# Second phase of a two-layer kernel: the 16 state products in four VectorE instructions, and new step orders

## The reference, cut to what matters

```
xa = layer_norm(x);  sx = (xa one token earlier) - xa
xxx = tanh((xa + sx*maa_x) @ maa_w1);  xm_f = xa + sx*(maa_f + xxx_f @ maa_w2_f)      # five mixes f
w = exp(-exp(time_decay + tanh(xw @ td_w1) @ td_w2))
r, k, v = xr @ Wr.T, xk @ Wk.T, xv @ Wv.T;   g = silu(xg @ Wg.T)
for t in tokens, per head:  a = k_t v_t^T;  out_t = r_t . (u*a + s);  s = a + w_t * s   # s is 16 x 16
og = group_norm(out);  x1 = x + (og * g) @ Wo.T
xc = layer_norm(x1);  xk2, xr2 = xc + (shift of xc) * ffn_k / ffn_r
result = x1 + sigmoid(xr2 @ Wfr.T) * (relu(xk2 @ Wfk.T)^2 @ Wfv.T)
```

## Time and profile before

| | |
|---|---|
| median of 3 runs | 1634.13 us (1631.69 to 1645.39) |
| the profiled execution's own time | 1638.29 us |
| its span, first to last instruction | 1636.5 us |
| busy share of the span: PE, DVE, ACT, POOL | 89%, 59%, 44%, 29% |
| mean granted TensorE clock | 0.965 |

### The profile page before, as it was taken

How to read it: one execution, slowest core, us unless ns; L and a number is a source line. 1 busy time by engine, 2 the same in 40 slices (tenths; PEclk the granted TensorE clock), 3 DMA queues, 4 the chain that set the end, 5 groups by cost and what they waited for, 6 DMA issues and landing times. The chain is left out here.

```text
span 1636.5 us, 33172 instructions
## 1 busy us (share of the span) xinstructions
PE 1455.7 (89%) x12352; PEld 1085.1 (66%) x12352; DVE 961.4 (59%) x2287; ACT 721.5 (44%) x1772; POOL 477.0 (29%) x530
## 2 busy tenths in 40 slices
PE   5999999999999998588989888889989888998865
PEld 4777777777777775376666666566656666666532
DVE  3444444444444434267787778777867867787652
ACT  3666666666666665124234423433342343334312
POOL 1211212221111110223453245224414523442230
PEclk9999999999999999599999999999999989999978
DMA  7431111111111000300000000000000000000000
GB/s 202 133 83 37 37 37 36 36 42 45 43 43 41 12 13 7 120 12 18 6 18 24 23 6 19 23 24 2 22 24 6 18 24 23 2 23 18 17 6 12
DMA packets 25664, 54.61 MB, mean 33 GB/s; under 512 B 3984, under 2 KB 6672, under 8 KB 24016
## 3 DMA queue, kind: packets, MB, share of 16 engines
q1 hardware_dynamic: 25552, 52.99, 11.3%
HBM read 42.23 MB, written 7.34 MB: 30 GB/s over the span
## 5 line engine op out<-in xcount | busy, mean ns | idle before, releaser
L900 POOL TENSOR_TENSOR rst<-rp,st 128x448 f32<-128x448 f32 x192 | 191.0, 1019 | 124.0 <-DVE st L1064 124.0
L892 POOL TENSOR_TENSOR xm<-mixed,xa 128x448 f32<-128x448 f32 x80 | 98.9, 1236 | 384.4 <-DVE mixed L993 382.7
L272 POOL TENSOR_TENSOR aT_lo<-whole,aT_hi 128x375 fp32r<-128x375 f32 x64 | 58.6, 915 | 448.4 <-ACT whole L424 445.6
L344 DVE CUSTOM_DVE_ANT_0 probs<-a_bank,unmask 112x375 f32<-112x375 f32 x256 | 126.0, 545 | 83.1 <-PE a_bank L541 72.4
L443 ACT ACTIVATE probs<-probs,least 112x375 f32<-112x375 f32 x256 | 153.8, 608 | 0.0
L350 DVE RECIPROCAL inv_rows<-sums 112x128 f32<-112x128 f32 x64 | 61.0, 953 | 155.9 <-ACT probs L443 155.9
L452 ACT COPY probsT<-a_bank 125x448 f32<-125x448 f32 x192 | 90.1, 536 | 52.1 <-PE a_bank L594 52.1
L594 PEld LDWEIGHTS a_bank<-ident_sb,probs 112*125 112x125 f32 x768 | 90.8, 188 | 30.9 <-ACT keyT L434 16.3
L594 PE MATMUL a_bank<-ident_sb,probs 112*125 112x112 f32 x768 | 99.3, 279 | 2.9 <-ACT probs L443 2.9
L993 DVE SCALAR_TENSOR_TENSOR mixed<-b_bank,vec_sb,sx 128x112 f32<-128x112 f32 x320 | 84.0, 323 | 21.0 <-PE b_bank L1476 20.9
L539 PE MATMUL a_bank<-aT_hi,wk_lo 128*128 128x376 f32 x256 | 91.3, 357 | 1.7 <-ACT keyT L434 1.7
(11 more groups left out here) (165 smaller groups left out, 3290.5 us busy)
## 6 DMA issues: line engine op xcount, KB each, us to landing
ctx_tok<-in_ctx SPq DMA_DIRECT2D x16, 750.0 KB
xT_sb<-in_xT SPq DMA_DIRECT2D x16, 224.0 KB, 9.5
x_tok<-in_x SPq DMA_DIRECT2D x16, 224.0 KB, 9.2
x_between_layers<-x_sb SPq DMA_DIRECT2D x16, 224.0 KB, 2.3
b_x<-x_between_layers SPq DMA_DIRECT2D x16, 224.0 KB, 2.8
x_post<-x_between_layers SPq DMA_DIRECT2D x16, 224.0 KB, 2.8
out_dram<-fin SPq DMA_DIRECT2D x16, 224.0 KB, 2.8
vbd<-vtok SPq DMA_DIRECT2D x208, 16.0 KB
```

The costliest lines, as they stand in the source:

```text
L344: dve.tensor_tensor_reduce(out=probs[:, g % 2, i], in0=score_bank[i][0:T, 0:TC], in1=unmask[:, m[1]], scale=-SCALE, scalar=-LOWEST, op0=AL ...
L892: pool.tensor_tensor(xm[:, f % 2], mixed[:, f % 2], xa[:, :, 1:T + 1], ALU.add).then_inc(s_xm, 1)
L900: pool.tensor_tensor(by_chunk(rst[:, j % NPROD]), by_chunk(rp[:].rearrange("p c t -> p (c t)")), state_of(j), ALU.mult).then_inc(s_pprod, 1)
```

## The change

- The tile `st` of the states and the tile `drep` of the decays are laid out with the state column outermost: [P, S, C, NB] in place of [P, C, S, NB]. The scan runs over the same 896 elements in the new order, and `drep` is filled by one ACT instruction instead of four.
- The 16 products become four, `products(m, r)`, all on DVE. Each multiplies four state columns at once, 128 x 1792 elements. POOL has no product any more. The ring has two places of four columns each, one semaphore `s_prod` counts the four instructions, and each `reduce` waits for one of them.
- The step functions of POOL, DVE, ACT and PE are written out as plain sequences without slots, in other orders. Some functions are cut in two so that their halves can stand apart (`chunk_keys`, `decay`, `copy_sums`, `residual`, `shift2`, `token_shift`). The work in them is the same. `tanh_gate` now also waits for the batch's own decay factors, and `transpose_value` for one more instruction of the earlier batch's near values.
- The program of SP is not touched.

```diff
-        drep = sb("drep", [P, C, S, NB])
+        drep = sb("drep", [P, S, C, NB])
...
-        st = sb("st", [P, C, S, NB])
+        st = sb("st", [P, S, C, NB])
...
-        rst = sb("rst", [P, NPROD, CT])
+        rst = sb("rst", [P, 2, QUAD, CT])
...
-        def state_of(j):
-
-            return st[:, :, j % QUAD * QUAD + j // QUAD, :].unsqueeze(3).broadcast_to([P, C, NB, CH])
+        def states_of(r):
+
+            return st[:, r::QUAD].rearrange("p q c b -> p q (c b)").unsqueeze(3).broadcast_to([P, QUAD, NG, CH])
...
-            def product(m, j):
-                if j == 0:
-                    pool.wait_ge(s_st, count(m, 1, 1))
-                    pool.wait_ge(s_rp, count(m, 1, 1))
-                if j >= NPROD or at_least(m, 1):
-                    pool.wait_ge(s_red, count(m, QUAD, (j - NPROD) // QUAD + 1))
-                pool.tensor_tensor(by_chunk(rst[:, j % NPROD]), by_chunk(rp[:].rearrange("p c t -> p (c t)")), state_of(j),
-                                   ALU.mult).then_inc(s_pprod, 1)
...
+                    rec_key(m)
+                if pre:
+                    mix(n, 0)
+                if more:
+                    rstd1(p)
+                if pre:
+                    mix(n, 1)
+                if post:
+                    gate_output(l, scan)
+                if pre:
+                    mix(n, 2)
+                    mix(n, 3)
+                if post:
+                    rstd2(l)
+                if pre:
+                    mix(n, 4)
+                if more:
+                    xa_state(p)
...
-            def product(m, j):
+            def products(m, r):
                 dve.wait_ge(s_st, count(m, 1, 1))
                 dve.wait_ge(s_rp, count(m, 1, 1))
-                if j >= NPROD or at_least(m, 1):
-                    dve.wait_ge(s_red, count(m, QUAD, (j - NPROD) // QUAD + 1))
-                dve.tensor_tensor(by_chunk(rst[:, j % NPROD]), by_chunk(rp[:].rearrange("p c t -> p (c t)")), state_of(j),
-                                  ALU.mult).then_inc(s_vprod, 1)
+                if r >= 2 or at_least(m, 1):
+                    dve.wait_ge(s_red, count(m, QUAD, r - 1))
+                dve.tensor_tensor(rst[:, r % 2].rearrange("p q (g s) -> p q g s", s=CH),
+                                  rp[:].rearrange("p c (b s) -> p (c b) s", s=CH).unsqueeze(1).broadcast_to([P, QUAD, NG, CH]),
+                                  states_of(r), ALU.mult).then_inc(s_prod, 1)
 
...
+                if scans:
+                    for d in range(2, CH + 1):
+                        decay_key(m, d)
+                    near_products(m, 0)
+                    prefixes(m)
+                if post:
+                    wkv_sum(l)
+                if scans:
+                    near_products(m, 1)
+                    decay_rec(m)
+                if more:
+                    stats1(p)
+                if scans:
+                    near_products(m, 2)
+                if post and at_least(n, 3):
+                    finish(later(n, -3))
+                if scans:
+                    near_products(m, 3)
+                if pre:
+                    mix(n, 0)
+                    mix(n, 1)
+                if post:
+                    centre(l)
+                if scans:
+                    scan(m)
+                    bonus_value(m)
+                    near_values(m, 0)
+                    products(m, 0)
+                    products(m, 1)
+                if post:
+                    group_norm(l)
+                if scans:
+                    products(m, 2)
+                if pre:
+                    mix(n, 2)
+                    mix(n, 3)
+                    mix(n, 4)
+                if scans:
+                    near_values(m, 1)
+                    near_values(m, 2)
+                if post:
+                    residual(l)
+                    stats2(l)
+                if scans:
+                    products(m, 3)
+                if post:
+                    apply2(l)
+                if more:
+                    apply1(p)
+                if scans:
+                    near_values(m, 3)
+                if post:
+                    shift2(l)
+                    ffn_input(l, xk2, "ffn_k", s_xk2)
+                    ffn_input(l, xr2, "ffn_r", s_xr2)
+                if more:
+                    token_shift(p)
+                if pre:
+                    gate(n)
+                if more:
+                    mix_input(p)
...
-                for c in range(C):
-                    last = act.copy(drep[:, c], prefix[:, c, 0:NB, CH].unsqueeze(1).broadcast_to([P, S, NB]))
-                last.then_inc(s_drep, 1)
+                act.copy(drep[:], prefix[:, :, 0:NB, CH].unsqueeze(1).broadcast_to([P, S, C, NB])).then_inc(s_drep, 1)
...
                     chunk_keys(m)
+                if pre:
+                    tanh_maa(n)
+                if scans:
+                    chunk_keys_decayed(m)
+                    copy_state(m)
+                    copy_keys(m)
                     spread_decay(m)
-                if pre:
-                    tanh_maa(n)
-                if scans:
-                    copy_keys(m)
+                    copy_sums(m, 0)
+                    copy_sums(m, 1)
+                if pre:
+                    tanh_td(n)
                 if post:
                     square(l)
-                if scans:
-                    copy_sums(m)
-                if post:
                     gn_rstd(l)
                 if pre:
-                    tanh_td(n)
+                    decay_rate(n)
+                    copy_value(n)
                 if post:
                     gn_affine(l)
                 if pre:
-                    decay(n)
-                    copy_value(n)
                     copy_key(n)
+                    decay_factor(n)
+                    copy_rec(n)
                 if post:
                     xc_affine(l)
-                if pre:
-                    copy_rec(n)
+                if more:
+                    xa_affine(p)
+                if pre:
                     tanh_gate(n)
-                    copy_vtok(n)
-                if pre and not is_batch(n, B - 1):
-                    xa_affine(later(n, 1))
                 if post:
                     relu_square(l)
                     receptance(l)
+                if pre:
+                    copy_vtok(n)
 
...
-                by_pool, by_vector = products(QUAD * r + QUAD - 1)
-                pe.wait_ge(s_pprod, count(m, POOL_PRODUCTS, by_pool))
-                pe.wait_ge(s_vprod, count(m, DVE_PRODUCTS, by_vector))
+                pe.wait_ge(s_prod, count(m, QUAD, r + 1))
...
-                    last = pe.matmul(out_bank[q * (P // QUAD):(q + 1) * (P // QUAD), 0:CT], collect[:, j], rst[:, j % NPROD],
+                    last = pe.matmul(out_bank[q * (P // QUAD):(q + 1) * (P // QUAD), 0:CT], collect[:, j], rst[:, r % 2, q],
...
+                if scans:
+                    transpose_keys(m)
+                if pre:
+                    maa_second(n, (0, 1))
+                if scans:
+                    chunk_sums_free(m)
+                if post:
+                    gn_mean(l)
+                if scans:
+                    chunk_sums(m)
+                    bonus(m)
+                if pre:
+                    decay_first(n)
+                if scans:
+                    attend_near(m, 0)
+                if pre:
+                    maa_second(n, (2,))
+                if scans:
+                    attend_near(m, 1)
+                if post:
+                    gn_var(l, scans)
+                if pre:
+                    decay_second(n)
+                    project(n, 1, "wv", s_vmm)
+                if scans:
+                    reduce(m, 0)
+                    attend_near(m, 2)
+                if pre:
+                    maa_second(n, (3, 4))
+                if scans:
+                    reduce(m, 1)
+                    reduce(m, 2)
+                if post:
+                    project_out(l)
+                if pre:
+                    project(n, 2, "wk", s_kmm)
+                if scans:
+                    attend_near(m, 3)
+                if pre:
+                    project(n, 3, "wr", s_rmm)
+                if post:
+                    transpose_post(l)
+                if more:
+                    transpose_x(p)
+                if scans:
+                    reduce(m, 3)
+                if pre:
+                    project(n, 4, "wg", s_gmm)
+                    transpose_value(n)
+                if post:
+                    ffn_key(l)
+                    ffn_receptance(l)
+                if more:
+                    maa_first(p)
+                if post:
+                    ffn_value(l)
```

More of the change, by code:

```diff
@@ L908, in step @@
                 if scan:
[L909 to L933, removed]
-                        pool.tensor_copy(xc[:, :, 0:1], rows[:, index(l), 0, :].unsqueeze(2)).then_inc(s_xc0, 1)
```

(39 more changed lines are left out.)

180 lines of the change are left out of this document (46 added, 134 removed).

## The result

The changed kernel takes **1697.93 us**, median of 4 runs (1697.23 to 1698.49); the kernel before, run beside it, 1639.76 us. The ratio is **1.0354** [1.029, 1.0417]. The profiled execution took 1698.49 us with a span of 1696.7 us, against 1638.29 and 1636.5 before: 60.2 us more.

The account below looks back on a forecast made before the run. PE, busy 89%, was taken as the bound, held each step through SP's queue. 1638.3 + 35 (longer steps) + 45.5 (clock) + 6 (steps 1 and 2) - 9 (last two) = 1716, as median 1712 us; range 1655 to 1745.

Parts of the forecast that it names:

- Where the wait is, and what causes it: PE before gn_mean: late copy_vtok and early stats1 meet in SP's queue, holding PE 9.4 us every step.
- V: The moment vtok is ready; b_x lands 12.46 us later, finish's first instruction ends 14.8 us later.
- What is late next: SP's queue: b_x behind 13 transfers delays stats1 and finish, closing the loop at 58.65 us a step.
- that case: Rival at gn_mean: SP's queue does not hold, steps take 49.3 us, about 1540 us in all; chance 8%.
- The four old waits: PE's waits for chunk sums, POOL product, DVE product and normalised input, 4.98 us a step, were to go.
- `reduce` 2 holds: On PE, product 2 ends at 31.8 us, wanted at 32.2: least slack, 0.4 us.
- Products: On DVE: each of 1792 elements takes at most 2.5 us, four take 10 against about 3 before.
- `ln_tok`: On DVE, rear part: 4.87 us beside POOL's products, 0.54 us once those go.
- walk of 42.35 us: PE's work from gn_mean to wfr without waits: 40.48 us plus one reduce (0.89) and bonus (0.98).
- The correction of 4.2 us: Whole kernel: the median of runs lies 4.2 us under the profiled execution, taking 1716 to 1712 us.
- The clock: PE behind its wait at gn_mean: falls to 0.50, costing 3.5 us a step, bounds 0 and 4.6.
- the first rival: At gn_mean: the same wait, but the clock hardly falls, 1663 us; chance 22%.

Follow-up runs that it names:

- the two moves alone: Kernel before with only copy_vtok put behind receptance on ACT and stats1 of the next batch ahead of finish on DVE: 1721.62 us, ratio 1.0533.
- both moves back: Changed kernel with copy_vtok returned to right behind tanh_gate on ACT and stats1 put behind centre on DVE: 1526.89 us, ratio 0.9308.
- PE kept busy: Changed kernel with eight unread matmuls on constants added on PE ahead of gn_mean's wait for the 13 transfers: 1660.56 us, ratio 1.0155.

## Why the prediction was right

It said 1712 us, 4.8% slower, in a range of 1655 to 1745; measured were 1697.93 us, 3.5% slower than the kernel before run beside it. The likeliest case, 1690 to 1727, is the one that came.

**Where the wait is, and what causes it: right.** It named `gn_mean` on the first instruction of `finish`, a stand of 9.4 us (9.30 measured), `b_x` issued 9.66 us behind the first transfer (9.66), DVE idle for about 12 us (12.35), `gn_mean` at V + 14.8 (14.87 as the mean of the 12 full steps, from the spread's start). Putting back either move takes away its share, freeing `b_x` in SP's queue does too, and the two moves alone slow the old kernel: the cause is shown, not argued. One remark of the prediction is too strong, that the rows contradict the sentence of the Trainium skill on the sequencer's time (DMA: Bandwidth & Descriptors, section "Issuing engines are not separate DMA queues"): a single issue, 0.67 us, is small beside the 2.8 us of a landing, and only the 13 in a row are not.

**What is late next: right.** With both moves back, PE does not stand at all in the full steps. The step was added up piece by piece (walked) at 49.3 us and measures 48.57. The time given for that case, 1540, was 13 us too long.

**The four old waits go, `reduce` 2 holds: right.** No such wait is left from 820 to 1560 us. **Products: right within the bound**; the upper end of 2.5 us was taken, 2.02 measured, as by the formula of the Trainium skill that the prediction cites (VectorE: DVE Perf Modes, section "The TRN2 errata"). **`ln_tok`: the sign was right, the size not**: 1.40 us in the row above instead of 0.54, and still far from 4.87; it cost nothing, since PE waits for something else.

**The pace, term by term**, mean of the 13 steps from 810.95 to 1602.37:

| term, us | predicted | measured | from |
|---|---|---|---|
| V to `gn_mean` | 14.8 | 14.53 | 12 steps at 14.87, the last, which loads no `b_x` any more, 10.47 |
| `gn_mean` to `wfv` at full clock | 44.18 | 43.46 | predicted 42.35 and `maa_first` 1.83; 886.15 to 929.61 with PE kept busy, clock 1.00 |
| slow clock in it | 3.5 | 3.12 | mean of the 13 in the changed kernel, 46.58, less 43.46 |
| `wfv` to the next V | -0.33 | -0.23 | the starts in SP's and PE's timelines |
| step | 62.15 | 60.88 | |

The split between the second and third row is rough: 43.46 is one full step, and the last of the 13 has less work (41.00 with PE kept busy). Over the same 13 steps the changed kernel's span is 3.27 us longer than with PE kept busy, where the clock fell in one step too.

So 13 steps came out 13 x 1.27 = 16.5 us shorter than forecast. Up to step 2 the change cost 2.3 us (810.95 against 808.62) where 6 was estimated, and behind the last spread it won 6.3 where 9 was. Together 1716 - 16.5 - 3.7 + 2.7 = 1698.5, the profiled time. The largest error is the **walk of 42.35 us**: PE's pieces between `gn_mean` and `wfr` take 41.60 us when nothing holds them. PE was busy for 40.33 us in that stretch of the kernel before, and one `reduce` and `bonus` add 1.87, which makes 42.2; where the remaining 0.6 us lie is open. The correction of 4.2 us from the profiled time to the median did not show again (1698.49 and 1697.93); it came from a median of three executions, where larger sets of the kernel before have medians of 1636.07 to 1639.99.

**The clock: right in kind and nearly in size.** Falling to 0.50 behind the stand, it cost 3.12 us a step: 2.3 in a step such as that of 887.46 (45.77 - 43.46), 4.4 in one such as that of 947.58 (47.83 - 43.46), and 1.4 in one (44.85 - 43.46). The bounds given were 0 and 4.6. That the 3.5, taken from a single row behind a pause of 2.27 us, came so near the mean is in part luck. The clock is about 40 of the 60 us; without it the change would have measured about what the first rival said, 1663 (1660.56 with PE kept busy).

**What it missed** is off this path. It counted what DVE's stalls beside POOL's products cost, and not what DVE's long products do to POOL. In the new orders that is covered (with both moves back PE is busy for 60.00 of 60 us); in the old ones it turned a win of 15 us (1622.86 against 1637.71) into a loss of 27 (1665.05 against 1638.21).

**What stays open:** the new step orders with the old sixteen products were not run, so how much of the 7% that the best version wins is the orders' and how much the products' is known only from the other side: products in the old orders win 0.9% at one choice of places and lose 1.7% at another.

## What to carry to other kernels

When a piece is moved forward in one engine's order and another backward in a second engine's, look for the queue where both meet: here SP's, where one load stood behind 13 transfers that took 8.66 us to issue, and the load's consumer stood in front of an instruction that PE needed. Put the consumer of a late load behind everything that others wait for, and the producer of a long burst of issues as early as its inputs allow. And price a longer instruction on DVE by what lies beside it on POOL, not only by its own length.

## What the runs showed of the hardware

- **The clock falls behind short pauses too, but not always.** Behind 1.82 us of waiting it fell (`gn_mean` 1.78 us, chunk sums 2.88), and in another step of the same kernel, behind 2.11 us, it did not (`gn_mean` 1.02). Behind 2.76 us `wo` kept full speed (3.69 us), and one step later behind 2.82 us it did not (6.56). With PE kept busy before it, a wait of 2.18 us did no harm, but behind one of 2.37 us four steps later the clock fell (`gn_mean` 1.86 us). The length of the last pause alone does not decide it in these runs.
- **The recovery takes mostly one of two lengths** after stands of nearly the same size: behind 9.30 us it was there 5 us after `gn_mean` began, behind 9.14 us nearly 10 us after. Of the 12 full spans from `gn_mean` to `wfv`, six take 47.5 to 47.9 us, five 45.6 to 45.9 and one 44.9.
- **A POOL operation that starts just behind the start of a long DVE product stands for all of it** in these runs, even a small one: 2.31 us for one element per partition in the changed kernel, where the same operation takes 0.54 to 0.57 us beside no product.

```profile
914.41 2.03 DVE L1059 TENSOR_TENSOR rst<-rp,st 128x1792 f32<-128x1792 f32 x1
```

```profile
914.53 2.31 POOL L894 TENSOR_TENSOR ln_rs<-ln_ve,neg_half 112x1 f32<-112x1 f32 x1 [5.36 <-DVE ln_ve L947]
```

- **An issue of a small transfer between two SBUF tensors took SP 0.67 us here** (8.66 / 13), while the load of 224 KB takes 0.33 us to issue (row 882.24).
